# Two routed adapter layers: whole down weights fetched and split first, up factors' differences on VectorE, biases and gains issued by SyncE

## What is computed

```
h = gelu(x @ W_down[role] + b_down[role])      # 1024 -> 512, exact gelu
y = x + h @ W_up[role] + b_up[role]            # 512 -> 1024
yn = (y - mean(y)) * rsqrt(var(y) + 1e-5)      # over the 1024 features
x = yn * gamma[role] + beta[role]
```

## Time and profile before

| | |
|---|---|
| median of 3 runs | 2823.11 us (2822.96 to 2826.91) |
| profiled execution | 2828.77 us |
| its span, first to last instruction | 2826.8 us |
| PE busy | 2711.9 us (96%), 11714 matmuls |
| DVE busy | 2159.2 us (76%) |
| ACT busy | 1689.6 us (60%) |
| POOL busy | 1422.4 us (50%) |
| mean granted TensorE clock | 0.982 |
| DMA | mean 203 GB/s |

### The profile page before, as it was taken

The page is one execution under the profiler, slowest core; times in us unless marked ns, Lnnn a source line. Parts: engine busy times, 40 slices in busy tenths (PEclk is TensorE's granted clock), DMA queues, the critical chain, the costliest instruction groups (busy, mean ns, idle before and its releaser), DMA issues.

```text
span 2826.8 us, 56889 instructions
## 1 busy us (share of the span) xinstructions
PE 2711.9 (96%) x11714; PEld 2216.2 (78%) x11714; DVE 2159.2 (76%) x3321; ACT 1689.6 (60%) x2907; POOL 1422.4 (50%) x956
## 2 busy tenths in 40 slices
PE   7899999998899999999989999999889999999997
PEld 5688888887788888888768888888667888888885
DVE  4677777766777777777788888888787888888886
ACT  3566666565565656666556565666555655656565
POOL 2455555555555555555454444444354444444446
PEclk9999999999999999999999999999999999999999
DMA  6565666666565656666666666656666666666663
GB/s 186 176 202 191 218 205 210 209 222 212 189 209 195 224 197 211 205 207 206 213 200 212 203 207 196 222 192 215 203 197 205 213 199 202 207 192 219 208 203 146
DMA packets 366261, 574.33 MB, mean 203 GB/s; under 512 B 41216, under 2 KB 241024, under 8 KB 365696
## 3 DMA queue, kind: packets, MB, share of 16 engines
q1 hardware_dynamic: 363968, 563.31, 61.5%
q0 software_dynamic: 1728, 6.29, 0.8%
HBM read 364.97 MB, written 204.47 MB: 201 GB/s over the span
## 4 chain that ended last, share of the span: by engine, by line
PE 82%; issue 7%; DVE 5%; POOL 1%; DVEq 1%; ACT 1%; DMA 1%; SPq 1%; POOLq 1%; ACTq 0%
PE pD L492 44%; PE bX L504 22%; PE bZ L504 16%; DVE xt L852 1%; DVE wul L769 1%; DVEq L222 1%; DVE hl L834 1%; DVE xt L875 1%; DVE wdl L752 0%; DVE xt L844 0%; DMA rwd<-in_Wd 0%; DVE xl L812 0%; POOL rwu L408 0%; POOL rwu L415 0%; ACT wdh L550 0%
## 5 line engine op out<-in xcount | busy, mean ns | idle before, releaser
L440 POOL TENSOR_TENSOR xt<-xt,cgb 128x1024 f32<-128x1024 f32 x260 | 699.8, 2692 | 342.9 <-ACT xt L662 341.6
L492 PE MATMUL pD<-wdh,xh 128*128 128x512 f32 x2080 | 818.9, 394 | 48.8 <-DVEq L796 40.4
L492 PE MATMUL pD<-wdl,xh 128*128 128x512 f32 x2080 | 815.1, 392 | 0.0
L492 PE MATMUL pD<-wdh,xl 128*128 128x512 f32 x2080 | 814.1, 391 | 0.0
L662 ACT ACTIVATE xt<-xt,rstd 128x1024 f32<-128x1024 f32 x260 | 298.9, 1150 | 383.1 <-POOL rstd L433 303.0
L492 PEld LDWEIGHTS pD<-wdh,xh 128*128 128x128 f32 x2080 | 394.6, 190 | 140.9 <-DVEq L796 49.5
L492 PEld LDWEIGHTS pD<-wdh,xl 128*128 128x128 f32 x2080 | 394.0, 189 | 83.0
L492 PEld LDWEIGHTS pD<-wdl,xh 128*128 128x128 f32 x2080 | 394.7, 190 | 81.4
L875 DVE SCALAR_TENSOR_TENSOR xt<-xt,nmean,cgb 128x1024 f32<-128x1024 f32 x260 | 441.4, 1698 | 0.0
L448 POOL TENSOR_TENSOR cs<-hT 128x256 f32<-128x256 f32 x130 | 97.1, 747 | 681.7 <-DVE hT L819 679.2
L504 PE MATMUL bX<-wuh,hh 128*128 128x512 f32 x1040 | 410.8, 395 | 27.7 <-DVE xt L844 21.5
(11 more groups left out here) (91 smaller groups left out, 3798.8 us busy)
## 6 DMA issues: line engine op xcount, KB each, us to landing
xq<-in_xB SPq DMA_DIRECT2D x130, 512.0 KB, 3.7
htok<-hg SPq DMA_DIRECT2D x260, 256.0 KB, 2.8
hq<-htok SPq DMA_DIRECT2D x1040, 64.0 KB, 2.3
xt<-in_x SPq DMA_DIRECT2D x130, 512.0 KB, 4.2
mid<-xt SPq DMA_DIRECT2D x130, 512.0 KB, 3.9
xq<-mid SPq DMA_DIRECT2D x520, 128.0 KB, 3.2
xt<-mid SPq DMA_DIRECT2D x130, 512.0 KB, 4.1
out<-xt SPq DMA_DIRECT2D x130, 512.0 KB, 2.7
```

The source lines that it names most:

```text
L440: eng.tensor_tensor(xt[:, k, :], xt[:, k, :], cgb[:, 1, :], ALU.add).then_inc(s_o, 1)
L492: last = eng.matmul(pD[e][:, :], a[:, e, 128 * k:128 * k + 128], w[:, k, :], start=False, stop=(k == 7 and n == 2), skip_group_check=True)
```

## The change

- `rwd` holds the whole down matrix. SP issues all eight transfers at once (`down_weights`) and then the bias; `down_rest` is gone, and `f_rd` counts once a matrix.
- `take_wd_1` becomes the first thing of `begin` on ACT, and on DVE it goes before the second item's `low_x`.
- On ACT, `take_wd_0` and the first `seed_d` go before the second `normal`, and `seed_x` goes before `seed_z` and waits for `s_cb`.
- The factor differences are done by DVE: the first two in a body of their own, `factors`, at the end of `begin` two steps after the down weights, the last two in `take_wu_1`. Factors 2 and 6 have a tile of their own, `twu`. DVE also makes the difference of the up bias.
- SP issues the up bias (`up_biases`) and gamma and beta (`gains`); POOL only waits for them. POOL's drains are gone.
- sqrt(1024) is multiplied into `rstd` by POOL in every step, not into gamma.
- ACT's and DVE's second loop makes ten turns (steps 70 to 129); SP's stays at nine.
- The scratch for DMAs issued by software gets 512 bytes (`dynamic_dma_scratch_size`).

```diff
-        rwd = sb("rwd", [128, 2, 2, K])
+        rwd = sb("rwd", [128, 8, K])
+        twu = sb("twu", [128, 2, 2, K])
...
-        def steps(eng, body, low, high):
+        def steps(eng, body, low, high, ahead):
+            for first in (6, NP + 5):
+                for c in range(low, first):
+                    body(Pair(c))
+                turns = (first // NP * NP + NP - ahead - first) // M
+                with eng.Fori(0, turns) as j:
+                    for m in range(M):
+                        body(Pair(first + m, j))
+                low = first + M * turns
+            for c in range(low, high):
                 body(Pair(c))
...
+            def down_weights(p):
+                row, c = adapter(p), pd.next()
+                eng.wait_ge(f_rd, c + 1)
+                for h in range(2):
+                    for a in range(4):
+                        r = 256 * a + 128 * h
+                        eng.dma_start(rwd[32 * a:32 * a + 32, 4 * h:4 * h + 4, :],
+                                      Wd[row, r:r + 128, :].rearrange("a (k i) n -> (a i) k n", i=32))\
+                           .then_inc(s_rd[h], 16)
                 count(eng, s_sd, p + -1, 2, 2)
                 eng.dma_start(cbd[:, :], bd[row, :].broadcast_to([128, K])).then_inc(s_bd, 16)
...
+            def up_biases(p):
+                row = adapter(p)
+                count(eng, s_sz, p + -1, 1, 1)
+                eng.dma_start(cbu[:, :], bu[row, :].broadcast_to([128, H])).then_inc(s_bu, 16)
+
+            def gains(p):
+                row = adapter(p)
+                count(eng, s_o, p + -1, 2, 2)
+                eng.dma_start(cgb[:, 0, :], ga[row, :].broadcast_to([128, H])).then_inc(s_gb, 16)
+                eng.dma_start(cgb[:, 1, :], be[row, :].broadcast_to([128, H])).then_inc(s_gb, 16)
...
                     eng.tensor_tensor(rstd[:, n:n + 2], var[:, n:n + 2], mhalf[:, 0:1].broadcast_to([128, 2]), ALU.pow)\
+                       .then_inc(s_rs, 1)
+                    count(eng, s_rs, p, 2, 1)
+                    eng.tensor_tensor(rstd[:, n:n + 2], rstd[:, n:n + 2], rooth[:, 0:1].broadcast_to([128, 2]), ALU.mult)\
                        .then_inc(s_rs, 1)
...
             def begin(i):
+                when_new(eng, i, take_wd_1)
                 high_x(i, 1)
                 gelu(i + -1, 1)
                 seed_d(i, 1)
                 high_h(i + -2, 0)
                 when_new(eng, i + -3, take_wu_2)
-                when_new(eng, i, take_wd_1)
...
                 high_h(w, 2)
-                normal(u + -1, 1)
-                seed_z(w)
-                seed_x(w)
                 when_new(eng, i + 1, take_wd_0)
                 seed_d(i + 1, 0)
+                normal(u + -1, 1)
+                seed_x(w)
+                seed_z(w)
                 when_new(eng, w, take_wu_1)
...
+            def factors(p):
+                c = pt.next()
+                eng.wait_ge(s_ru, c * 128 + 128)
+                eng.tensor_tensor(b12, b12, b11, ALU.subtract).then_inc(s_sub, 1)
+                eng.wait_ge(s_sub, c * 4 + 1)
+                eng.tensor_tensor(t2, b22, b12, ALU.subtract).then_inc(s_sub, 1)
+                eng.wait_ge(s_sub, c * 4 + 2)
+                eng.sem_inc(s_seen, 1)
...
             def take_wu_1(p):
                 c = pg[1].next()
-                low_wu(c * 7, 2, b12)
+                low_wu(c * 7, 2, t2)
                 low_wu(c * 7, 3, b22)
+                eng.tensor_tensor(t4, b21, t2, ALU.subtract).then_inc(s_sub, 1)
+                eng.wait_ge(s_wul, c * 7 + 1)
+                eng.tensor_tensor(b11, t2, b11, ALU.subtract).then_inc(s_sub, 1)
...
                 onto(u, 1, bX[u.c % 2], 0, 0)
+                when_new(eng, i, take_wd_1)
+                ready(i, s_wd[1])
                 low_x(i, 1)
                 onto(u, 2, bZ, 1, 1)
+                low_h(w, 0)
                 when_new(eng, u, take_wu_2)
                 ready(u, s_wu[2])
-                when_new(eng, i, take_wd_1)
-                ready(i, s_wd[1])
-                low_h(w, 0)
+                when_new(eng, w, factors)
```

More of the change, by code:

```diff
@@ L122, in routed_adapters @@
             "s_it", "s_io", "s_id", "s_p", "s_oh", "s_pc", "s_ctl"))
-        s_rd = [sem(f"s_rd{k}") for k in range(3)]
+        s_rd = [sem(f"s_rd{k}") for k in range(2)]
         s_ru = sem("s_ru")
@@ L245, in routed_adapters @@
         b11, b12, b21, b22 = (rwu[:, g, :, n, :] for g in range(2) for n in range(2))
+        t2, t4 = (twu[:, n, :, :] for n in range(2))
         block = ctx.enter_context(nc.Block())
@@ L377, in step @@
                 store(z, 1)
-                when_new(eng, i + 1, down_rest)
+                when_new(eng, u, gains)
                 if (i + 1).first():
                     up_weights(i + 1)
-            steps(eng, step, -1, NPH + 4)
+                    up_biases(i + 1)
+                if not v.first():
+                    when_new(eng, v, up_biases)
+            steps(eng, step, -1, NPH + 4, 2)
             for k in range(XB):
@@ L455, in step @@
             def step(i):
[L456 removed]
+                w, z = i + -2, i + -4
                 sums(w)
[L458 to L467 removed]
+                if z.exists():
+                    when_new(eng, z, take_gb)
+                    eng.sem_inc(s_cg, 1)
+                norm(z)
+                shift(z, 0)
+                shift(z, 1)
             plain_steps(eng, step, 0, NPH + 4)
@@ L548, in high_wd @@
                 count(eng, s_Db, p + -1, 4, q + 1)
[L549 to L550 removed]
+                eng.wait_ge(s_rd[q // 2], c * 64 + 64)
+                eng.activation(wdh[:, 2 * q:2 * q + 2, :], rwd[:, 2 * q:2 * q + 2, :], ACT.Copy).then_inc(s_wdh, 1)
             def take_wd_0(p):
@@ L621, in seed_x @@
                 if p.exists():
+                    count(eng, s_cb, p, 1, 1)
                     count(eng, s_v, p + -2, 7, 7)
@@ L659, in normal @@
                     n, k = 2 * (p.c % 2) + e, p.slot(e)
-                    count(eng, s_rs, p, 1, 1)
+                    count(eng, s_rs, p, 2, 2)
                     count(eng, s_n, p, 2, e + 1)
@@ L692, in end @@
                 square(u, 1, 1)
-            steps(eng, halves(begin, end), -1, NPH + 5)
+            steps(eng, halves(begin, end), -1, NPH + 5, 0)
         @block.vector
@@ L900, in end @@
                 ready(w, s_wu[0])
+                ready(w, s_cb)
                 last_onto(u, 4, bZ, 0, 1, 3)
```

109 lines of the change are left out of this document (22 added, 87 removed).

## The result

| | before | after |
|---|---|---|
| median, us | 2823.03 (2821.42 to 2826.91, 4 runs) | 2803.5 (2800.72 to 2804.2, 4 runs) |
| profiled execution | 2828.77 | 2803.86 |
| its span | 2826.8 | 2802.0 |
| mean granted clock | 0.982 | 0.987 |

The ratio is 0.9926, 95% interval 0.9911 to 0.994: 19.5 us faster. The profiled execution of before lay 5.7 above its median, that of after on its own, so the two traces differ by 24.8.

The account below looks back on a forecast made before the run. TensorE bounds ordinary steps, 20.40 us without idle time; gains lie at weight changes, loop turns and start. -7 - 5 - 6.5 + 5 = -13.5 from the profiled 2828.77 gives 2815.3, less 5.7 is 2810; range 2795 to 2824.

Parts of the forecast that it names:

- the likeliest case: Whole kernel: the forecast itself, 2810 us, faster than before; chance 0.52.
- Down: Steps 30, 65, 95, where down weights change: release wait replaced by a stall at the first `bX` matmul; -7 us.
- early-bias rival: Down changes: bias transfer does not wait for all eight, a change costs 3 instead of 10; total 2796; chance 0.14.
- Up: Steps after a down change, where up weights follow: differences on DVE, the 4.64 us release wait replaced by 3.4; -5 us.
- Start: Kernel start: earlier first add cuts the 6.11 us stall to 3.5, the release wait behind it shrinks by 2; -6.5 us.
- Loops: Layer 1's loop turns: one jump more, 2.0, and POOL's multiply of `rstd`, 0.3 after each of nine jumps; say +5 us.
- dear multiply: POOL's multiply in every step costs 1.67 us like the power, so layer 1's steps lose; total 2842; chance 0.11.
- The second half is not early: Down changes: ScalarE's conversions stand behind late squares, so the second-half waits stay; priced at 2822, no chance of its own.

Follow-up runs that it names:

- b1: Changed kernel with the bias `cbd` issued after four of the eight down-weight transfers, not after all: 2798.3 us, ratio 0.9909 to before.
- e1: Changed kernel with VectorE's check, work and release of the down weights' second half back behind the last up group, `low_h` after them: 2829.14 us, ratio 1.0027 to before.
- c4: Changed kernel with the four differences of the up factors made on POOL again: 2807.08 us, ratio 0.994 to before.
- c1: Changed kernel with sqrt(1024) multiplied into gamma at each load again, not into `rstd` in each step: 2795.34 us, ratio 0.9897 to before.
- c2: Changed kernel with ScalarE's check and work for the down weights' second half moved behind its `high_x` of the second item: 2796.6 us, ratio 0.9907 to before.
- c3: Changed kernel with VectorE's check, work and release of the down weights' second half behind the last up group and behind `low_h`: 2895.97 us, ratio 1.0253 to before.
- e3: Changed kernel with edits of b1, c1 and c2, ScalarE's old order of normalisation and seeds, and thirty-step loop turns on ScalarE and VectorE: 2772.45 us, ratio 0.9822.
- b4: Changed kernel with loops of twelve steps a turn on ScalarE and VectorE: 2788.39 us, ratio 0.9869 to before.

## Why the prediction came out as it did

The direction, the likeliest case and its places were right; 2810 was 6.5 too high, inside the range. That it came so near is in part luck: by the traces the terms were 11.3 too small together (-13.5 for -24.8), and 5.7 taken off for the profiled execution of before hid half of it. By its terms:

- **Down, -7 forecast, -9.1 measured.** The mechanism is as it stood there: no release wait but 0.66, and a stall at the first `bX` matmul, with 2.45, 3.06 and 7.02 for "near 3" (7.2 less the 3.4 of its own working is 3.8), a short one, and 7.2. Step 95 gave 0.7 (nothing forecast), steps 30 and 65 gave 4.4 and 3.9 for 5 and 2. The early-bias rival is refuted by the trace of after, and b1 shows what it is worth when made true: 5.6, not 14. The seed of `pD` in ScalarE's timeline of after, before the normalisation and the seed of `bX` that PE's step 95 waits for:

```profile
1999.97 0.60 ACT L588 ACTIVATE pD<-cbd 128x512 f32<-128x512 f32 x1 [3.97 <-DMA cbd<-in_bd]
```

- **Up, -5 forecast, -15.7 measured: the term that was mis-sized.** In steps 96 to 98 the waits were 5.86, 1.01 and 2.35 for 5.6, 1.8 and 3.4, and the excess 13.6 for 16. Two things failed. The third-add wait that takes the place of the 4.64 was taken 1.0 to 1.7 us too long: 1.70, 1.95 and 2.35 in steps 33, 68 and 98 for 3.4. And step 32 was given the fourth-add wait of layer 1, 5.6, where it was 1.80: there VectorE's pair took 2.35, not 4.49, as POOL's shift falls elsewhere. So the excess was 9.0 for 14. What I had not asked is what the release's place is worth by itself: e1 puts 13 us of the up changes on it, c4 7 on the differences. That is more than the 15.7, so the two overlap or hold some of the 1 to 3 us of the places; how the 15.7 divides between them is open.
- **Start, -6.5 forecast, -10.4 measured.** The 6.11 became 3.04 (3.5 forecast), the release wait of 4.58 behind it went altogether, where I had it shrink by 2; a wait of 1.22 for the third add stands there now.
- **Loops, +5 forecast, +11.1 measured.** The multiply is 0.20 us, as taken, and ordinary steps stayed at 20.40: the dear multiply is refuted. But a turn rose from 1.9 to 2.6, where I had 0.3 for it. c1 shows that the multiply has 0.5 of a turn, and c2 what was left out: ScalarE's check ahead of `high_x`, which I had put among those that cost nothing because they run ahead behind queued work. Before a jump VectorE waits for what it holds up, and nothing covers that. The turn of step 99 costs 4.0, since it meets adds that are still late from the up change.
- **Not in the sum:** small losses in layer 0, -2.9 (its turns now cost in steps 11 and 35 alone, 1.7 together, where before 13 steps lost 0.2 to 0.5 each), and the end, +2.2, mostly the multiply (1.6 by c1, and the sorting of the ends above).

The errors have both signs: start, down, up and layer 0 came out 19.6 better, loops and end 8.3 worse. The rest of the difference is the base: I took 5.7 for what the profiled execution lay above its median, and the profile of after shows no such excess.

**The second half is not early** was priced at 2822. e1 makes its waits true, by another cause, and takes 2829. The places of e1 against those of before are start -6.7, down +1.5 and up -2.5, near the -6.5, 0 and 0 of the price. The trace of e1 is 0.6 above that of before, where the price had 1.5 below: the rest of layer 1 is +9.8 for the +5 of the loops, layer 0 -3.3, the end +1.8. The other 5 of the 7 us are what the profiled execution of before lay above its median, and that of e1 did not.

## What to carry to other kernels

Where an engine releases something in every step that another waits for, its place in the order is worth more than the work around it: here the whole gain is gone when one exchange of lines on VectorE is undone, and one place further down (c3) the kernel is 72 us slower than before. Whether that exchange would bring the gain alone no run shows. Before costing a check or a small operation at nothing, look for the places where its cover is gone, as on either side of a loop's jump, and count them. Edits that work on the same place (the turn) are to be summed there, not each by its own gain.

## What was unexpected of the hardware

- A loop's jump holds VectorE for some 3.3 us. The stretch without VectorE work between the last of `begin` and the first add of `end` is 0.50 us in step 74 of e1, and 3.78 in step 75, where the jump lies in it:

```profile
1582.59 0.69 DVE L834 TENSOR_TENSOR xt<-bX,xt 128x512 f32<-128x512 f32 x1 [0.50 <-PE bX L475]
```
```profile
1606.29 0.69 DVE L834 TENSOR_TENSOR xt<-bX,xt 128x512 f32<-128x512 f32 x1 [3.78 <-PE bZ L475]
```

In after it is 1.40 in step 77 and 4.80 in step 75, with more checks in it. At step 99 it is longer with thirty steps a turn (e3, second row) than with six (after, first row), but the twelve-step turns of b4 have 4.2 to 4.7, no more than the six-step ones: that it grows with the loop's body is not shown.

```profile
2113.37 0.69 DVE L834 TENSOR_TENSOR xt<-bX,xt 128x512 f32<-128x512 f32 x1 [5.28 <-issue]
```
```profile
2095.77 0.69 DVE L832 TENSOR_TENSOR xt<-bX,xt 128x512 f32<-128x512 f32 x1 [5.82 <-issue]
```

The page's queue of instruction loads moved 3.79 MB in after and 3.16 MB in e3:

```profile
q14 instruction: 463, 3.79, 0.5%
```
```profile
q14 instruction: 386, 3.16, 0.4%
```

The Trainium skill (Runtime: NRT & Kernel Launch, on instruction fetch mechanics) says that a taken branch to a place outside the loaded window waits for a fetch. Fewer turns with fewer loads agree with that; that the fetch is what VectorE waits for, no run here shows by itself.

- POOL's multiply of 128x2 took 0.195 us where the power on the same tile takes 1.67: what a small POOL operation costs goes by its kind. In four of 130 times it took 0.61 to 1.22; the 1.15 at 680.46 began 0.12 us after VectorE's pair at 680.34.
